# Attention: probabilities split into halves before they are turned, and turned by one DMA a head instead of ten TensorE transposes

## The reference

```python
q, k = rope(x @ Wq.T), rope(x @ Wk.T)          # 32 and 8 heads of 128, RoPE in the rotate-half form
v = x @ Wv.T
p = softmax(causal_mask(q @ k.T / sqrt(128)))
y = (p @ v) @ Wo.T
```

## Time and profile before

| | us |
|---|---|
| median of 3 runs (2484.25 to 2486.66) | 2485.41 |
| the profiled execution | 2484.75 |
| its span, first to last instruction | 2482.8 |
| TensorE busy in the span | 2378.8 (96%) |
| VectorE busy | 1787.9 (72%) |
| ScalarE busy | 1591.7 (64%) |
| GpSimd busy | 1232.0 (50%) |

### The profile page before, as it was taken

How to read it: one execution, slowest core, us unless ns; L and a number is a source line. 1 busy time by engine, 2 the same in 40 slices (tenths; PEclk the granted TensorE clock), 3 DMA queues, 4 the chain that set the end, 5 groups by cost and what they waited for, 6 DMA issues and landing times. The chain is left out here.

```text
span 2482.8 us, 48888 instructions
## 1 busy us (share of the span) xinstructions
PE 2378.8 (96%) x15424; PEld 1368.9 (55%) x15624; DVE 1787.9 (72%) x3234; ACT 1591.7 (64%) x3327; POOL 1232.0 (50%) x986
## 2 busy tenths in 40 slices
PE   6999999999999999999999998879999999999797
PEld 3555555555555555555555555445555555555443
DVE  6777777777777777777777776577777777788522
ACT  7676776776776776776776775265665656656422
POOL 4455555555555556556556459344434343454223
PEclk8999999999999999999999999999999999999999
DMA  7343343343343343343343341230110110100000
GB/s 248 108 129 111 108 128 111 108 133 105 113 132 107 110 133 109 106 137 109 102 140 109 119 151 56 103 124 1 43 43 1 44 44 1 43 18 1 1 0 34
DMA packets 113827, 218.79 MB, mean 88 GB/s; under 512 B 9632, under 2 KB 43040, under 8 KB 111360
## 3 DMA queue, kind: packets, MB, share of 16 engines
q1 hardware_dynamic: 113536, 215.28, 26.6%
HBM read 212.10 MB, written 3.15 MB: 87 GB/s over the span
## 5 line engine op out<-in xcount | busy, mean ns | idle before, releaser
L256 DVE SCALAR_TENSOR_TENSOR xc<-bank,taps,xc 128x511 f32<-128x511 f32 (+2 forms) x384 | 284.7, 742 | 44.6 <-ACT xc L243 27.4
L984 ACT ACTIVATE E<-wq,cst 128x128 f32<-128x128 f32 x1024 | 311.8, 390 | 2.2 <-PEq L298 2.2
L1268 POOL TENSOR_TENSOR xw<-xt,wdec 128x384 f32<-128x384 f32 x128 | 106.4, 832 | 327.3 <-DVE xt L1119 163.7
L1277 POOL TENSOR_TENSOR acc<-acc,sq 128x512 f32<-128x512 f32 x112 | 172.0, 1536 | 186.8 <-ACT sq L996 186.8
L1911 POOL TENSOR_TENSOR qT<-qT,qrot 128x512 f32<-128x512 f32 x64 | 81.3, 1270 | 368.6 <-DVE qrot L1801 368.6
L1161 DVE SCALAR_TENSOR_TENSOR u<-xc,D,bank 128x512 f32<-128x512 f32 x128 | 95.6, 747 | 210.3 <-PE bank L813 198.8
L1100 DVE TENSOR_TENSOR E<-E,cbm 128x1024 f32<-128x1024 f32 x128 | 242.9, 1898 | 0.8
L61 PE MATMUL bank<-xhi,wx 128*128 128x512 f16 x640 | 242.5, 379 | 0.0
L60 PE MATMUL bank<-xlo,wx 128*128 128x512 f16 x640 | 242.5, 379 | 0.0
L59 PE MATMUL bank<-xhi,wx 128*128 128x512 f16 x640 | 242.5, 379 | 0.0
L1263 POOL TENSOR_TENSOR ecs<-ecs,xcC 128x768 f32<-128x768 f32 x128 | 234.1, 1829 | 0.4 <-POOLq L298 0.4
(11 more groups left out here) (237 smaller groups left out, 6299.4 us busy)
## 6 DMA issues: line engine op xcount, KB each, us to landing
wq<-cs_rows SPq DMA_DIRECT2D x128, 512.0 KB, 4.1
ecs<-ecs_rows SPq DMA_DIRECT2D x128, 384.0 KB, 3.6
wx<-in_w_xbc SPq DMA_DIRECT2D x80, 256.0 KB, 2.7
wz<-in_w_z SPq DMA_DIRECT2D x64, 256.0 KB, 2.7
wo<-in_w_o SPq DMA_DIRECT2D x64, 256.0 KB, 4.0
wq<-in_wq SPq DMA_DIRECT2D x8, 1024.0 KB, 5.7
awo<-in_wo SPq DMA_DIRECT2D x8, 1024.0 KB, 5.0
wkv<-in_wkv SPq DMA_DIRECT2D x8, 512.0 KB, 3.7
```

The source lines that it names most:

```text
L256: self.nc.vector.scalar_tensor_tensor(out=dst[:, d:T], in0=self.k.bank[bank][:, 0:T - d], scalar=self.taps[:, bass.ds(g, 1), b, j, 3 - d:4 ...
L984: ins = nc.scalar.activation(E[t.i % 4][:, h, c], sc.csr[t.i % 2][:, h, c * P:(c + 1) * P], ACT.Relu, scale=-1.0, bias=head(sc.cst, t, c, h))
L1277: nc.gpsimd.tensor_tensor(acc[t.b][:], acc[t.b][:], sq[:], ALU.add).then_inc(acc_done, 1)
```

## The change

The probabilities are now split first, and both halves are turned together by one DMA.

- ScalarE's `normalise` writes the leading half in fp16 into `phalves` instead of fp32 in place (`leading_p`). VectorE then computes probability x reciprocal - leading half, in fp16, into the same buffer (`rest_of_p`), four instructions of 128 to 512 columns. The 20 blocks of 128x128 lie in an order that lets each of these write with a fixed step. There are two buffers `phalves`.
- SP starts one `dma_start_transpose` a head, `phalves` to `pturned` (128 x 20 x 128, fp16), when `rest_of_p` of this head and `attend` of the head before are done. `attend` waits for the DMA (`pt_in`). There is one buffer `pturned`.
- The ten transposes, ScalarE's three copies and VectorE's three subtractions from PSUM are gone. There is one fp32 buffer `probs`; the exponentials of a head wait for `rest_of_p` of the one before.
- Banks 5 and 6 join the ring of projections: RING = (0, 1, 5, 6), and TensorE waits for the use before the last three.
- V is no longer copied to SBUF first. ScalarE copies its leading half from the bank and VectorE subtracts it there, after ScalarE; GpSimd has no part in it.
- The weights of the last stage are loaded in steps, one a head, through groups 0 and 1. `dscale` is loaded at the start of the last stage.

```diff
@@ attention, SP
+                def turn(n, h):
+                    sp.wait_ge(p_lo, n + 1)
+                    sp.sem_inc(step, 1)
+                    if not (isinstance(n, int) and n == 0):
+                        sp.wait_ge(pv_ready, n)
+                        sp.sem_inc(step, 1)
+                    sp.dma_start_transpose(out=pt[:], in_=ph[h % 2][:]).then_inc(pt_in, 16)
...
-                load_swiglu(k, io, sp)
+                turn(0, 0)
...
+                            if later(g, b, h, 1):
+                                turn(n + 1, h + 1)
+                            if isinstance(g, int) and g < 2:
+                                load_swiglu(k, io, sp, n)
@@ TensorE
+        def ring_free(pe, ahead):
+            wait(pe, proj_free, ahead - 3)
...
                 def attend(n, g, b):
                     pe.wait_ge(pv_free, n + 1)
+                    pe.wait_ge(v_lo, (g * NB + b) + 1)
+                    pe.wait_ge(pt_in, 16 * n + 16)
                     for j in range(CH):
-                        pe.wait_ge(pt_lo, 3 * n + min(j, 2) + 1)
-                        if j == 0:
-                            pe.wait_ge(kv_lo, 2 * (g * NB + b) + 2)
-                        ps = slice(T_OFF[j], T_OFF[j] + T - j * P)
-                        mm = product(nc, k.bank[7][:, j * P:T], (vhi[b][:, j], vlo[b][:, j]), (pthi[:, ps], ptlo[:, ps]),
-                                     j == 0, j == CH - 1)
+                        out = k.bank[7][:, j * P:T].rearrange("p (i t) -> p i t", t=P)
+                        mm = product(nc, out, (vhi[b][:, j], vlo[b][:, j]),
+                                     (pt[:, 6 * j + 1:5 * j + 5], pt[:, 6 * j:16 + j:5]), j == 0, j == CH - 1)
...
-                            turn(n, h, [0], None)
-                            turn(n, h, [1], None)
...
-                                pe.wait_ge(proj_free, ahead - 1)
+                                ring_free(pe, ahead)
...
-                            turn(n, h, [2, 3], 3 * n + 1)
@@ ScalarE
                 def exps(n, h):
                     act.wait_ge(nmax_done, n + 1)
+                    wait(act, p_lo, n)
...
-                def normalise(n, h):
+                def leading_p(n, h):
                     act.wait_ge(exp_done, n + 1)
                     act.wait_ge(rsum_done, n + 1)
+                    wait(act, pt_in, 16 * n - 16)
                     for i in range(CH):
-                        s = slice(P_OFF[i], P_OFF[i] + (i + 1) * P)
-                        ins = nc.scalar.activation(pr[h % 2][:, s], pr[h % 2][:, s], ACT.Copy, scale=rsum[h % 2][:, i:i + 1])
-                    ins.then_inc(norm_done, 1)
+                        nc.scalar.activation(leading_blocks(h, i), probs(i), ACT.Copy,
+                                             scale=rsum[h % 2][:, i:i + 1]).then_inc(p_hi, 1)
...
+                def leading_v(u, b, ahead, bank):
+                    act.wait_ge(proj_ready, ahead + 1)
+                    nc.scalar.copy(vhi[b][:], bank[:, :].rearrange("p (t d) -> p t d", d=P)).then_inc(kv_hi, 1)
@@ VectorE
-                        nc.vector.tensor_copy(v[:], k.bank[bank][:, :].rearrange("p (t d) -> p t d", d=P)).then_inc(v_ok, 1)
-                        dve.wait_ge(v_ok, u + 1)
+                        dve.wait_ge(kv_hi, 2 * u + 2)
+                        nc.vector.tensor_tensor(vlo[b][:], bank[:, :].rearrange("p (t d) -> p t d", d=P), vhi[b][:],
+                                                ALU.subtract).then_inc(v_lo, 1)
...
-                def rest_of_p(n, u):
-                    bank, at, size = EVAC[u]
-                    dve.wait_ge(pt_hi, 3 * n + u + 1)
-                    nc.vector.tensor_tensor(ptlo[:, at:at + size], k.bank[bank][:, 0:size], pthi[:, at:at + size],
-                                            ALU.subtract).then_inc(pt_lo, 1)
+                def rest_of_p(n, h):
+                    for i in range(CH):
+                        dve.wait_ge(p_hi, 4 * n + i + 1)
+                        out = ph[h % 2][:, 5 * i * P:(6 * i + 1) * P].rearrange("p (b t) -> p b t", t=P)
+                        ins = nc.vector.scalar_tensor_tensor(out=out, in0=probs(i), scalar=rsum[h % 2][:, i:i + 1],
+                                                             in1=leading_blocks(h, i), op0=ALU.mult, op1=ALU.subtract)
+                    ins.then_inc(p_lo, 1)
```

More of the change, by code:

```diff
@@ L1513, in attention @@
         krot = sb("krot", [P, T])
-        pr = [sb(f"probs{i}", [P, 1280]) for i in range(2)]
+        pr = sb("probs", [P, 1280])
         qhi, qlo = ([sb(f"q{n}{i}", [P, T], F16) for i in range(4)] for n in ("hi", "lo"))
@@ L1518, in attention @@
         vhi, vlo = ([sb(f"v{n}{i}", [P, CH, P], F16) for i in range(NB)] for n in ("hi", "lo"))
-        pthi, ptlo = sb("pthi", [P, 1280], F16), sb("ptlo", [P, 1280], F16)
+        ph = [sb(f"phalves{i}", [P, P_BLOCKS * P], F16) for i in range(2)]
+        pt = sb("pturned", [P, P_BLOCKS, P], F16)
         ohi, olo = ([sb(f"o{n}{i}", [P, QH, T], F16) for i in range(NB)] for n in ("hi", "lo"))
@@ L1593, in _ @@
                 aw.load_wo(sp, 1, 1)
-                load_swiglu(k, io, sp)
+                turn(0, 0)
                 def body(g, s, p):
[L1598 to L1603, removed]
+                    for b in range(NB):
+                        for h in range(QH):
+                            n = item(g, b, h)
+                            if later(g, b, h, 1):
+                                turn(n + 1, h + 1)
+                            if isinstance(g, int) and g < 2:
+                                load_swiglu(k, io, sp, n)
+                            if b == 0 and h == QH - 1 and not (isinstance(g, int) and g in (0, NG - 1)):
+                                sp.wait_ge(proj_ready, ring(g, 0, QH - 1, 1)[0] + 1)
+                                aw.load_wo(sp, g + 1, 1 - s)
+                            if b == 1 and h == 0 and not (isinstance(g, int) and g >= NG - 2):
+                                sp.wait_ge(proj_ready, ring(g, 1, 0, 0)[0] + 1)
+                                aw.load(sp, g + 2, s)
                 pairs(sp, body)
@@ L1612, in project @@
                             w = wq[s][:, kt, h * P:(h + 1) * P] if kind == "q" else wkv[s][:, kt, 0:P]
-                            mm = product(nc, k.bank[bank][:, :], (lead(w), rest(w)), (k.xhi[:, kt, x], k.xlo[:, kt, x]),
+                            mm = product(nc, bank[:, :], (lead(w), rest(w)), (k.xhi[:, kt, x], k.xlo[:, kt, x]),
                                          kt == 0, kt == KT - 1)
@@ L1662, in output @@
                         w = wo[s][:, h]
-                        mm = product(nc, k.bank[bank][:, :], (ohi[b][:, h, x], olo[b][:, h, x]), (lead(w), rest(w)),
+                        mm = product(nc, bank[:, :], (ohi[b][:, h, x], olo[b][:, h, x]), (lead(w), rest(w)),
                                      h == 0, h == QH - 1)
@@ L1767, in body @@
                             n = item(g, b, h)
[L1768 to L1772, removed]
+                            if later(g, b, h, 1):
+                                leading_p(n + 1, h + 1)
                             if later(g, b, h, 3):
@@ L1859, in _ @@
                         dve.wait_ge(q_lo, 1)
-                    serve("q", 2 + h, h % 2, h, 0, 0, h)
+                    serve("q", 2 + h, k.bank[RING[(2 + h) % 4]], h, 0, 0, h)
                 maxima(0, 0)
                 scales(0, 0)
+                rest_of_p(0, 0)
                 maxima(1, 1)
@@ L1871, in body @@
                                 scales(n + 1, h + 1)
-                            for u in range(2):
-                                rest_of_p(n, u)
                             for i, (kind, what) in enumerate(uses):
@@ L1878, in body @@
                                     serve(kind, ahead, bank, n + 3, 0, what[1], what[2])
-                                elif kind != "o":
+                            if later(g, b, h, 1):
+                                rest_of_p(n + 1, h + 1)
+                            for i, (kind, what) in enumerate(uses):
+                                ahead, bank = ring(g, b, h, i)
+                                if kind in "kv":
                                     serve(kind, ahead, bank, 0, g * NB + b + 1, what[1], 0)
-                            rest_of_p(n, 2)
                             if later(g, b, h, 2):
@@ L1929, in _ @@
                 add_q(1, 1)
-                rest_of_v(0, 0)
                 rest_of_q(1, 1)
```

126 lines of the change are left out of this document (58 added, 68 removed).

## The result

The changed kernel takes 2633.28 us (median of 4 runs, 2631.57 to 2636.99) against 2486.03 us before (4 runs beside them, 2484.25 to 2489.18): 1.059 times as long, 95% interval 1.057 to 1.061, or +147 us. The forecast was 2648, +163.

A forecast was written before the change was run, and what follows sets the result against it. TensorE's instruction order bound the old kernel; the ring through VectorE and ScalarE would bind the new one. Eight heads at 109.1 us against 88.7, eight times the difference, +163 us on 2484.75, gave 2648 us; range 2425 to 2850.

The forecast's parts named there:

- The ring through VectorE and ScalarE: Attention head: maximum row, exponentials, sums, VectorE's ordered work to the next maximum; a plain head at least 7.5 us + R.
- Plain head with a split: Five of eight heads, GpSimd also splitting a weight: R 5.6 us, the head 13.1 us.
- Plain without a split: One of eight heads, only GpSimd's addition and qlo in the way: R 3.9 us, the head 11.4 us.
- KV head: Second head of each unit of four, where K and V are also projected; two of eight, 16.1 us each.
- the wait for vhi: KV head: VectorE stands still about 2.6 us for ScalarE's copy of V, behind K's copy and GpSimd's addition of K.
- Eight heads: One group of the attention stage: 5 x 13.1 + 11.4 + 2 x 16.1 = 109.1 us, against 88.7 before.
- R: Time of VectorE's four rest_of_p instructions in a head: 1.9 us with nothing in the way, more beside GpSimd.
- the taking of turns with GpSimd: VectorE instructions with two SBUF inputs share a port with GpSimd; each GpSimd instruction of d us costs VectorE d - 0.2.
- Rival 1: In rest_of_p VectorE keeps the port, only GpSimd's addition comes first: R 3.0 in all heads, 2537 us; chance 0.13.
- Rival 2: GpSimd does not block rest_of_p: R 1.9, 2466 us, or 2415 if V's wait is hidden; chance 0.21.
- rival 3: The DMA transpose, if above 11.2 us, sets every head's period: 2986 us at 17 us, 2794 at 14; chance 0.22.
- a period of P hide a transfer of P - 1.9: DMA transpose between attends: attend takes 1.9 us, the rest of the head's period hides the transfer, up to 11.2 us.

The follow-up runs named there:

- e1: Changed kernel with GpSimd's addition of Q's rotation, weight split and qlo all held until VectorE's four rest_of_p instructions are done; 2503.82 us.
- e2: Changed kernel with only GpSimd's weight split and qlo held behind rest_of_p, the addition of Q staying where it was; 2545.91 us.
- e6: Changed kernel with every transposing DMA made twice, the second after the first has landed; 2685.22 us.
- e9: Changed kernel with every transposing DMA made three times in a row; 2968.82 us.
- e4: Changed kernel with the edits of e1 and e3 together; 2479.37 us, 0.997 of the kernel before.
- e8: e4 with GpSimd's split and klo held for the reciprocal, addition of Q behind rest_of_p, qlo behind nmx, two splits moved to other heads; 2449.55 us.
- e3: Changed kernel with ScalarE copying V before K; 2599.57 us.

## Why the prediction was right

**What binds.** The ring through VectorE and ScalarE took TensorE's place, as forecast. TensorE's idle time stands before khi,qhi with the exponentials as releaser, and one gap of it is 4.08 us ("some 4 us"):

```profile
1881.09 0.58 PE L59 MATMUL bank<-khi,qhi 128*128 128x512 f16 x1 [4.08 <-ACT probs L1743]
```

**The terms.** Plain head with a split: forecast 13.1 us, measured 12.81. Plain without a split: forecast 11.4, measured 11.16. The second to fourth row here are the two sums that bound that head and its rest_of_p, 3.73 us (forecast 3.9); the first is where the eight heads below begin:

```profile
1799.85 0.17 DVE L1847 TENSOR_SCALAR sums<-sums 128x4 f32<-128x4 f32 x1 [1.02 <-ACT probs L1743]
...
1841.25 0.17 DVE L1847 TENSOR_SCALAR sums<-sums 128x4 f32<-128x4 f32 x1 [1.02 <-ACT probs L1743]
...
1843.94 3.73 DVE L1855 SCALAR_TENSOR_TENSOR phalves<-probs,rsum,phalves 128x128 f16<-128x128 f32 x4 [0.24 <-ACT phalves L1754]
...
1852.41 0.17 DVE L1847 TENSOR_SCALAR sums<-sums 128x4 f32<-128x4 f32 x1 [1.02 <-ACT probs L1743]
```

KV head: forecast 16.1, measured 15.74, with rest_of_p 2.85 (3.0) and the wait for vhi 2.51 (2.6). Eight heads run from the sums at 1799.85 to those at 1906.58, 106.7 us, where 109.1 was forecast and 88.7 stood before: 8 x 18.0 = 144 of the measured 147 us. The forecast lies 2.4 us a group above, most of it in R; it also counts sixteen KV heads where there are fifteen.

**The size that was a little off.** R beside a split was taken as 1.9 plus 3.73 = 5.6 and was 5.39: a GpSimd instruction costs VectorE a little less than its time less 0.2. Free of GpSimd R is 1.94 us (e1), as worked out.

**Rivals.** Rival 1 (only the addition comes first) fell: a split stands between two of VectorE's four instructions. e2 made it by hand, 2545.91 us where it was priced at 2537. Rival 2 (no blocking) fell by e1. The DMA transpose of rival 3 landed in 4.9 us, near the bound from the plain copies (4.3), far from the upper one (17) and farther from the estimate of 26 us for twenty blocks in series.

**What the prediction had wrong without harm.** It let a period of P hide a transfer of P - 1.9, 11.2 us in these heads. That takes attend's end as the start of every transfer; in most heads rest_of_p ends later, and 6.3 us are left in the head shown. With 4.9 us the transfer was hidden all the same, with 1.4 us to spare and not 6: that it was right here is in part luck, and a transfer of 7 to 11 us, which it would have called hidden, would not have been in such a head. It held TensorE's clock at full through the gaps (0.90 in the window), which cost nothing while TensorE waited anyway, but showed in e6 and e9. And it treated the taking of turns with GpSimd as a matter of instructions with two operands in SBUF. nmx has one, and pays too when a GpSimd instruction starts first. In e1 that makes 37 of the 39 us missed; in e2 and e4 it is the likely reason. e8, which moves GpSimd away from nmx as well, came at 2449.6 us, at the upper end of the 2435 to 2450 expected; it moves other things too, so that its gain over e4 is not nmx's alone.

**Where the gain went.** Ten transposes a head were 70 us of TensorE. The same change made VectorE read both operands from SBUF at the moment when GpSimd starts, and put V's subtraction behind ScalarE's copy. The first costs more than the gain (e1: 129 us), the second 34 (e3). With both out of the way the DMA transpose pays, 36 us of the 70 (e8). The rest is what TensorE, with 8.58 us of its own in a plain head of 9.57, still waits: for the ring, and in about equal part for klo.

## What to carry to other kernels

When an operand moves from PSUM to SBUF, list what GpSimd starts at the same moment, and price each of its instructions at nearly its full duration on VectorE's path (here 0.91 us for an addition of 1.27); then look where VectorE works from PSUM or waits, and put GpSimd there by a wait. After moving it, look at the small instructions at the new place, too. A shorter engine is worth only the distance to the next ring, so work out that ring, instruction by instruction, before removing work from the engine that binds. And to see what a transfer may take, look for the last of the things that start it, not for the period.

## What the runs showed of the hardware that was not expected

- A 128x4 fp32 tensor_scalar within SBUF, 0.17 us alone, took 0.84 to 1.00 us where a GpSimd instruction of 1.16 us had started ahead of it, and ended within 0.02 us of it (e1, e2). The maxima, which read PSUM, took 1.67 us both with a GpSimd split beside them and without.
- The transposing DMA of 640 KB from SBUF to SBUF landed 4.9 us after its issue, about what a plain load takes (512 KB in 3.7, 1024 KB in 5.7), and held the issuing queue for 3.0 to 3.1 us.
- Attends that began behind idle times of 3.33 us (e6, at 1905.17) and 7.20 us (e9, at 1917.71) ran at a granted clock of 0.50, 1.2 GHz: 3.15 us in e9 instead of 1.86. One behind 1.11 us (e6, at 1890.16) ran at 1.00.
